# Graph network kernel on one core: a wait for the landing of each group of four gathers in the second layer

## What is computed

```
edge_index = jnp.stack([src, dst])
h = jnp.maximum(_layernorm(x, axis=-1), 0.0)
x = x + _L0_gnn_ref(h, edge_index)
h = jnp.maximum(_layernorm(x, axis=-1), 0.0)
x = x + _L1_gnn_ref(h, edge_index, edge_weight, L1_gnn_W, L1_gnn_b)
...
x = x + _L2_gnn_ref(h, L2_gnn_W_self, L2_gnn_W_neigh, src, dst)
...
x = x + _L3_gnn_ref(h, edge_attr_64, src, dst, ...)
```

```
norm = dinv[row] * w * dinv[col]
h = x @ W
msg = h[row] * norm[:, None]
out = jax.ops.segment_sum(msg, col, num_segments=n)
return relu(out + b)
```

## Time and profile before

| what | us |
|---|---|
| median of 3 runs | 1106.03 |
| lowest and highest | 1105.96, 1106.82 |
| profiled execution, first to last instruction (its span) | 1325.8 |
| second layer in it, from the first gather at 334 | to 640 |
| last layer in it | about 716 to 1325.8 |

### The profile page before, as it was taken

The page is one execution under the profiler, slowest core; times in us unless marked ns, Lnnn a source line. Parts: engine busy times, 40 slices in busy tenths (PEclk is TensorE's granted clock), DMA queues, the critical chain, the costliest instruction groups (busy, mean ns, idle before and its releaser), DMA issues.

```text
span 1325.8 us, 24512 instructions
## 1 busy us (share of the span) xinstructions
PE 1006.6 (76%) x6145; PEld 618.1 (47%) x6145; DVE 830.9 (63%) x2605; ACT 452.6 (34%) x1035; POOL 592.2 (45%) x763
## 2 busy tenths in 40 slices
PE   3788887996667767667696787777787878777685
PEld 2566553553444545445355444434444534444443
DVE  8988877357645556757657554565555555555556
ACT  3677771011434333334013232232232323222232
POOL 6533330000665666654003656555555555555550
PEclk9677778998887788877797899999888998999997
DMA  2000006001111111100523533333333333333331
GB/s 54 2 0 0 0 0 243 1 1 22 24 23 19 20 21 22 21 19 17 168 63 75 138 81 79 76 76 76 77 73 77 75 71 77 75 73 78 72 75 34
DMA packets 145110, 72.80 MB, mean 55 GB/s; under 512 B 111917, under 2 KB 136698, under 8 KB 144922
## 3 DMA queue, kind: packets, MB, share of 16 engines
q1 hardware_dynamic: 127224, 54.98, 16.0%
q0 software_dynamic: 16448, 16.88, 6.9%
q10 hardware_dynamic: 1378, 0.22, 0.1%
HBM read 59.66 MB, written 12.35 MB: 54 GB/s over the span
## 4 chain that ended last, share of the span: by engine, by line
PE 41%; another core or an unknown queue 20%; issue 16%; DVE 12%; ACT 6%; DVEq 2%; POOL 1%; ACTq 1%; DMA 1%; SPq 1%; POOLq 0%
PE seg L1628 10%; PE big L1658 5%; PE big L1552 4%; PE seg L1683 4%; PE seg L1755 3%; PE big L1791 3%; PE seg L1802 2%; ACT A L1345 2%; PE seg L1566 2%; PE big L1781 1%; ACT A L1466 1%; PE seg L1696 1%; ACT A L1472 1%; PE seg L1823 1%
## 5 line engine op out<-in xcount | busy, mean ns | idle before, releaser
L1221 POOL DMA_INDIRECT A<-table,idx x338 | 327.3, 968 | 260.6 <-ACT idx L1317 154.2
L1221 POOL DMA_INDIRECT pair<-table,idx x176 | 176.2, 1001 | 126.8 <-ACT idx L1317 65.0
L1755 PE MATMUL seg<-A 128*128 128x384 f16 (+1 forms) x624 | 137.6, 370 | 44.5 <-issue 19.1
L1466 ACT COPY A<-big 128x512 f32<-128x512 f32 x104 | 61.1, 587 | 249.7 <-remote 156.7
L1345 ACT CAST A<-big 128x500 f32 x208 | 125.4, 603 | 48.0 <-PE big L1557 25.9
L1791 PE MATMUL big<-A 128*128 128x512 f32 x208 | 114.1, 631 | 33.6 <-ACT A L1466 28.3
L2033 DVE COPY A<-seg 128x512 f32<-128x512 f32 x52 | 36.0, 691 | 162.3 <-remote 150.6
L1683 PE MATMUL seg<-A,cur 128*64 128x160 f32 x750 | 94.8, 353 | 46.0 <-issue 45.9
L1397 ACT COPY A<-big 128x500 f32<-128x500 f32 x120 | 66.5, 576 | 181.4 <-remote 113.8
L1755 PEld LDWEIGHTS seg<-A 128*128 128x128 f16 x624 | 60.3, 106 | 140.5 <-issue 91.0
L1658 PE MATMUL big<-A 128*128 128x300 bf16 x480 | 106.1, 367 | 18.8 <-issue 10.4
(11 more groups left out here) (307 smaller groups left out, 1809.6 us busy)
## 6 DMA issues: line engine op xcount, KB each, us to landing
A<-in_edge_attr_dram SPq DMA_DIRECT2D x103, 128.0 KB
A<-drel_flat SPq DMA_DIRECT2D x104, 126.0 KB
spilled_adjacency<-A SPq DMA_DIRECT2D x1, 7074.0 KB, 21.8
A<-spilled_adjacency SPq DMA_DIRECT2D x6, 1152.0 KB, 11.8
A<-table,idx POOLq DMA_INDIRECT x338
A<-pr_table SPq DMA_DIRECT2D x104, 31.5 KB
pair<-table,idx POOLq DMA_INDIRECT x176
A<-low_flat SPq DMA_DIRECT2D x78, 32.0 KB
```

The lines of the kernel that those rows point to most:

```text
L1221: pool.indirect_dma_start(out=row(q, j), out_offset=None, in_=table, in_offset=bass.IndirectOffsetOnAxis(ap=idx[:, q, j:j + 1], axis=0)).t ...
L1466: nc.scalar.copy(x_t[:, r, :], big[:, r, :]).then_inc(x_t_ready[r], 1)
L1755: op = nc.tensor.matmul(made[:, 0:held.shape[2] * D], hot_low[:, u, m, :], held[:, k, :, :], start=(m == 0 and k == 0), stop=(m == 3 and k ...
```

## The change

The function `gathers`, which served both layers, is split. A helper `group` issues the four (or three) gathers of a group as before. `gathers1` serves the second layer: it is a plain Python loop, so its 44 groups are written out in GpSimd's code instead of looped over, and ahead of every group but the first it has one more wait, for the semaphore `gathered` of the group before it to reach the count at which its four gathers have all landed. `gathers3` serves the last layer and is as before.

```diff
-            def gathers(g, row, slot_free):
-
-                pool.wait_ge(table_stored, 32 * (g + 1))
-                with pool.Fori(0, (IT1, IT)[g]) as it:
+            def group(it, q, row):
+                pool.sem_inc(gathers_begun, 1)
+                for j in range(G):
+                    if row is not row1 and q in MADE and j == 2:
+                        continue
+                    pool.indirect_dma_start(
+                        out=row(q, j), out_offset=None, in_=table,
+                        in_offset=bass.IndirectOffsetOnAxis(ap=idx[:, q, j:j + 1], axis=0)).then_inc(gathered[q], 16)
+
+            def gathers1():
+                pool.wait_ge(table_stored, 32)
+                for it in range(IT1):
                     for q in range(Q):
-                        pool.wait_ge(idx_ready[q], g * IT1 + it + 1)
-                        slot_free(it, q)
-                        pool.sem_inc(gathers_begun, 1)
...
+                        pool.wait_ge(idx_ready[q], it + 1)
+                        rows_summed(it, q)
+                        if it or q:
+                            pool.wait_ge(gathered[(q - 1) % Q], (it + (q > 0)) * (16 * G))
+                        group(it, q, row1)
+
+            def gathers3(row):
+                pool.wait_ge(table_stored, 64)
+                with pool.Fori(0, IT) as it:
+                    for q in range(Q):
+                        pool.wait_ge(idx_ready[q], IT1 + it + 1)
+                        rows_transposed(it, q)
+                        group(it, q, row)
...
-            gathers(0, row1, rows_summed)
+            gathers1()
...
-            gathers(1, lambda q, j: X[:, q, j, 0:D], rows_transposed)
+            gathers3(lambda q, j: X[:, q, j, 0:D])
```

More of the change, by code:

```diff
@@ L1208, in pool_link @@
                 pool.wait_ge(pool_chain, pool_links[0])
-            def gathers(g, row, slot_free):
-                pool.wait_ge(table_stored, 32 * (g + 1))
-                with pool.Fori(0, (IT1, IT)[g]) as it:
-                    for q in range(Q):
-                        pool.wait_ge(idx_ready[q], g * IT1 + it + 1)
-                        slot_free(it, q)
-                        pool.sem_inc(gathers_begun, 1)
[L1218 to L1223, removed]
+            def group(it, q, row):
[9 more added lines that the diff above has]
+                for it in range(IT1):
+                    for q in range(Q):
+                        pool.wait_ge(idx_ready[q], it + 1)
[10 more added lines that the diff above has]
+                        group(it, q, row)
             def rows_summed(it, q):
```

## The result

The changed kernel takes 1193.76 us (median of 4 runs, 1192.33 to 1194.36) against 1106.42 us for the kernel before (4 runs, 1105.96 to 1107.99). The ratio is 1.0784, with a 95% interval from 1.0769 to 1.0799: 87 us slower. The forecast was 1165 us, 59 us slower, with a range up to 1193 us. The measured time lies 0.8 us outside of it.

What follows compares the result with a forecast made beforehand. The chain of gathers was to become layer 2's bound: 43 x 7.0 + 4.9 + 1.55 = 307 us against 247 before, 60 us longer, so 1106 + 60 = 1166, said as 1165 us; range 1110 to 1193 us.

Steps and rivals of the forecast that it cites:

- The landing as read from the earlier trace: Layer 2: from the end of a group's last gather to ScalarE's start on its rows, 1.50 to 1.55 us.
- The loop's removal: Layer 2's gathers: taking away the hardware loop with its branch and register instructions gives 0.
- the 2 us that were allowed for it: Written-out code of 44 groups, about 75 more rows on GpSimd: taken as 0, at most 2 us.
- the gap: GpSimd's idle time between two groups in layer 2: 2.1 us with the wait (1.5 to 2.35), against 0.30 us.
- the length before: Layer 2, first gather to weighing of the last group, before the change: 247 us, between 231 and 296 us.
- GpSimd's 0.80 us: Time GpSimd takes from a semaphore to a gather, read at an index copy: 0.80 us.
- upper end of 318 us: Longest chain, first gather to last weighing, with the waits: 43 x 7.25 in the sum; 307 us was expected.
- the two cases that were set out: Profiled layer 2 grows about 15 us but median 60: unprofiled layer was shorter; both grow 15: first rival holds.
- a sign of being wrong: Prediction wrong if the gap is under 1 us, or TensorE's "issue" idle time in layer 2 shrinks by tens of us.
- the first rival: Layer 2 really lasts the profiled 306 us, so GpSimd's idle time hides most waits: 1109 to 1129 us; chance 0.26.
- The second rival: The wait doesn't bind, since the landing comes before GpSimd would have gone on: 1106 us, within 0.2%; chance 0.05.
- The third: Rival: faster, as a shallower gather queue gives back part of TensorE's crawl in layer 2: 1092 us; chance 0.07.

Runs made afterwards that it cites:

- second profile of before: The unedited kernel before, profiled a second time: 1106.2 us in one run, with a profile span of 1104.4 us.
- 87 waits: The changed kernel with a second wait inside each group, after its second gather: 1257.05 us, ratio 1.1359.
- shift of 16 gathers: Kernel before with IT1 = 10, FIRST_EARLY = 5 (160 gathers instead of 176): 1114.46 us; with its sums also spread to step 60: 1099.12 us.

## Why the prediction was right in kind and short in size

**The mechanism held.** The chain of gathers becomes longer by 43 waits, nothing hides them, ScalarE stands at its weighing 43 times, and every engine behind it waits. The landing as read from the earlier trace rows (1.50 to 1.55 us) is 1.51 us in the changed kernel. The loop's removal was taken at 0, and measured at 0 without the waits; with them, the one gap of 2.05 us inside a group lies within the 2 us that were allowed for it. What failed is the size of two terms of the sum, the gap and the length before.

**The gap was too small.** I took 2.1 us out of 1.5 to 2.35, with the argument that ScalarE's own start is contained in the 1.55 us. The measured gap is 2.35 us: the landing and GpSimd's 0.80 us add up in full. That is 43 x 0.25 = 11 us. The records are as long as taken (175.9 us against 176.2), but the gaps inside the groups come to 2.5 us more than 132 x 0.30 us, 1.7 us of it in the one ahead of the 114th gather. So the chain is 320.4 instead of 307 us, 13 us more. Even the upper end of 318 us was passed by 2 us: the gap came out at its own upper end, and the gaps inside a group had been given none.

**The length before was too long.** The 247 us came from shrinking 295.6 us evenly by 0.834. The true chain is 233.7 us, near the 231 us that I gave as the least possible. This is the other 13 us: 60 + 13 + 13 = 86. The even shrinking had no ground in any row. The rows had more to offer: TensorE's need of 197 us lay under GpSimd's 229 us, so if TensorE's crawl belonged to the excess of the profile, GpSimd's 65.0 us of waits for index copies went with it, and 295.6 - 65.0 = 231 us is the lower end.

**The range was missed by 0.8 us only.** Its top of 87 us was the longest chain less the shortest length before, 318 - 231. Both extremes came, 320.4 - 233.7 = 86.7 us. That the two overshoots of 2 to 3 us cancel is luck; the range had no room for either.

**Two signs named in the prediction misled.** The profiled chain grew by 25 us (295.6 to 320.4) and the median by 87, which fits neither of the two cases that were set out, though it is nearer to the first. And TensorE's idle time by "issue" before the weight loads of `apply_block` did shrink by tens of us, from 71.5 us to 20.4 us, which was named as a sign of being wrong. But it is 16.3 us in the second profile of before, so the drop is the disturbance's and not the change's (first row the changed kernel, second row before):

```profile
PEld seg L1695 <- issue: 20.4, 45, 0.6
PEld seg L1683 <- issue: 16.3, 46, 0.6
```

**The time of the first rival** (1120 us, by the starts of the profile) would have been far off. The profile of before was of a disturbed execution, as its 1325.8 us against a median of 1106.03 us warned, and by it TensorE seemed to set the pace where GpSimd did. The argument against this rival was misread, too: "the rest of the span shows no such holes" is wrong, since the page of the same profile has 154.2 us of GpSimd's waits for index copies in the last layer. The second rival falls by the gaps of 2.35 us. The third falls by the second profile of before, which has no crawl, and by the times with 43 and 87 waits, which grow by as much as the chain of gathers.

**The Trainium skill's price** for one DMA of this kind (DMA: Bandwidth & Descriptors, section "Anatomy of one DMA — SWDGE (gpsimd) path") would have made the gap 1.9 us. The trace has 2.35 us. Its 2.08 us from issue to completion are also under the 1.02 + 1.49 = 2.51 us from the start of a gather's record to ScalarE's start in the changed kernel, so the measured time decides.

## What to carry to other kernels

- Where the profiled execution is much longer than the timed runs, don't scale it evenly; profile it again if you can. Otherwise work out each engine's own need from its undisturbed records. Here the longest of these was GpSimd's 229 us, which no wait of the profile pointed to, and it was the bound in the timed runs.
- A wait for the landing of a small DMA, placed on the engine that issues a bound chain of DMAs, costs the landing and the restart, each time (2.03 us each for 43 waits). Where another engine is the bound, it costs only what it adds beyond that bound (60 instead of 89 us with three gathers in a group). The same wait one group later is free.
- Moving work off a bound engine pays only if the order of the others is spread anew: the same shift of 16 gathers cost 8.5 us with the old spacing and gave 8 us with a new one.

## What the runs showed of the hardware

- The order in which three waits are written ahead of a gather on GpSimd is worth 0.5 to 0.6 us for each gather that waits: 1190.63 us with the landing awaited last, by a separate instruction (mean gap 2.29 us), and 1165.51 us with it first, carried by the gather (1.77 us).
- In the second profile of before a gather of 128 rows of 256 bytes takes up 1.25 us of GpSimd at best and 1.32 us in the mean (176 in 232 us). ScalarE starts on the rows it waited for mostly 1.4 to 1.6 us after the gather's record ends (mean 1.51 us in the changed kernel, the longest 2.1 us). With four, three or two gathers between two waits, the mean gap at a group's start is 2.35, 2.37 and 2.37 us.
- One and the same program left a profile of 1325.8 us and another of 1104.4 us, with timed runs near 1106 us. In the longer one TensorE crawled in stretches of about 10 us within layer 2, and two thirds of the excess lay in the last layer. The cause stays open.
